# A fourth column group in fp16 pairs, with its high half subtracted by the matrix engine

## The reference

```python
def gnn(x, adj, W, a):                     # called with layernorm(x)
    Wh = x @ W
    e = leaky_relu((Wh @ a[:256])[:, None] + (Wh @ a[256:])[None, :], 0.2)
    e = where((adj > 0) | eye, e, -9e15)
    return softmax(e, axis=1) @ Wh

def ffn(x, Wr, br, ln_g, ln_b, W1, b1, W2, b2):   # called with layernorm(x)
    top_p, top_idx = top_k(softmax(x @ Wr + br), 2)
    weights = top_p / top_p.sum(-1)
    xe = normalised(x) * ln_g[e] + ln_b[e]        # for each expert e
    y = gelu(xe @ W1[e] + b1[e]) @ W2[e] + b2[e]
    return sum of weights * y over the two experts

x = x + gnn(layernorm(x), adj, W, a)
x = x + ffn(layernorm(x), ...)
```

## Time and profile before

| | us |
|---|---|
| median of 3 runs | 986.12 (984.92 to 988.51) |
| the profiled execution's own time | 986.23 |
| its span, first to last instruction | 984.5 |
| PE busy | 950.2 (97%) |
| DVE busy | 780.9 (79%) |
| POOL busy | 687.1 (70%) |
| ACT busy | 615.3 (63%) |

### The profile page before, as it was taken

The page is one execution under the profiler, slowest core; times in us unless marked ns, Lnnn a source line. Parts: engine busy times, 40 slices in busy tenths (PEclk is TensorE's granted clock), DMA queues, the critical chain, the costliest instruction groups (busy, mean ns, idle before and its releaser), DMA issues.

```text
span 984.5 us, 23001 instructions
## 1 busy us (share of the span) xinstructions
PE 950.2 (97%) x7562; PEld 800.1 (81%) x7563; DVE 780.9 (79%) x1199; ACT 615.3 (63%) x905; POOL 687.1 (70%) x726
## 2 busy tenths in 40 slices
PE   6999999999999999999999999999999999999994
PEld 5788999899888998998898977777777777777773
DVE  6789989999999999999999446787666666667653
ACT  4889898897788887977787454333333433343441
POOL 5222261498886987887869558888888888788763
PEclk9999999999999999999999999999999999999998
DMA  9658979688788687886876996442332332233221
GB/s 267 135 158 233 294 229 279 202 270 234 223 254 294 195 287 233 249 263 175 256 273 188 364 356 207 92 114 59 61 56 44 48 59 43 43 48 50 36 43 22
DMA packets 92637, 170.71 MB, mean 173 GB/s; under 512 B 20480, under 2 KB 69888, under 8 KB 84224
## 3 DMA queue, kind: packets, MB, share of 16 engines
q1 hardware_dynamic: 57984, 133.54, 40.6%
q0 software_dynamic: 24048, 26.23, 16.9%
q10 hardware_dynamic: 10512, 9.72, 3.4%
HBM read 136.65 MB, written 41.19 MB: 181 GB/s over the span
## 4 chain that ended last, share of the span: by engine, by line
PE 48%; ACT 1%; issue 1%; DMA 0%; DVE 0%; POOLq 0%; ACTq 0%; DVEq 0%
PE acc L934 12%; PE tp L913 7%; PE tp L915 6%; PE tp L914 6%; PE acc L937 6%; PE acc L807 2%; PE tp L784 2%; PE xt_ps L887 2%; PE acc L804 1%; PE acc L803 1%; PE acc L805 1%; PE rt_ps L827 0%; DMA out<-y_sb,yidx 0%; ACT hf L1177 0%; PE xt_ps L816 0%
## 5 line engine op out<-in xcount | busy, mean ns | idle before, releaser
L566 POOL TENSOR_TENSOR x_late<-x_late,wsp 128x256 f32<-128x256 f32 x128 | 149.6, 1198 | 126.3 <-DMA x_late<-in_L_ffn_W 92.8
L1177 ACT ACTIVATE hf<-tp,b_cols 128x256 f32<-128x256 f32 (+1 forms) x312 | 116.1, 459 | 174.7 <-PE tp L915 172.2
L804 PE MATMUL acc<-wh,pt_hi 128*128 128x256 f16 x768 | 209.3, 273 | 0.0
L803 PE MATMUL acc<-wh,pt_hi 128*128 128x256 f16 x768 | 209.3, 273 | 0.0
L805 PE MATMUL acc<-wh,pt_lo 128*128 128x256 f16 x768 | 209.3, 273 | 0.0
L934 PE MATMUL acc<-w_sb,h_hi 128*128 x568 | 170.9, 379 | 0.7 <-DVE h_lo L1615 0.6
L1311 DVE SCALAR_TENSOR_TENSOR sc<-t_row,s_col 128x2048 f32<-128x2048 f32 x64 | 159.2, 2487 | 10.2 <-PE tp L784 8.3
L913 PE MATMUL tp<-x_hi,w_sb 128*128 128x256 f16 (+1 forms) x624 | 162.4, 264 | 1.9 <-ACT hf L1177 1.8
L673 POOL DMA_INDIRECT out<-y_sb,yidx x71 | 120.7, 1700 | 60.5 <-DVE y_sb L1635 34.4
L915 PE MATMUL tp<-x_down,w_sb 128*128 128x256 f16 (+1 forms) x624 | 162.5, 264 | 0.0
L914 PE MATMUL tp<-x_lo,w_sb 128*128 128x256 f16 (+1 forms) x624 | 161.9, 263 | 0.0
(11 more groups left out here) (238 smaller groups left out, 1785.7 us busy)
## 6 DMA issues: line engine op xcount, KB each, us to landing
adj_sb<-in_adj SPq DMA_DIRECT2D x64, 1024.0 KB, 6.6
x_late<-in_L_ffn_W SPq DMA_DIRECT2D x32, 512.0 KB, 8.2
wsplit_dram<-wsp SPq DMA_DIRECT2D x32, 512.0 KB, 7.0
w_sb<-wsplit_dram SPq DMA_DIRECT2D x32, 512.0 KB, 9.5
xs<-rows_dram ACTq DMA_DIRECT2D x32, 260.0 KB, 3.2
wsp<-in_L_ffn_W POOLq DMA_DIRECT2D x32, 256.0 KB, 5.1
x<-in_x SPq DMA_DIRECT2D x32, 128.0 KB, 8.1
out<-x SPq DMA_DIRECT2D x32, 128.0 KB
```

What stands on the lines that cost most here:

```text
L566: ins = pool.tensor_tensor(wf[q][:, cols], wf[q][:, cols], wsp[q][:, cols], ALU.subtract)
L803: pe.matmul(o, pt_hi[g][:, cols], wh[:, j, 0, :], start=(j == 0), stop=False)
L804: pe.matmul(o, pt_hi[g][:, cols], wh[:, j, 1, :], start=False, stop=False)
```

## The change

The fourth column group is split into fp16 halves like the others, so `Wh` has a low half for all 32 row tiles and `wh32` and `pt32` go. Its low half is not made by DVE. PE subtracts the high half in PSUM: two matmuls of 512 columns with a stationary matrix `minus`, minus the identity divided by 1024, add to the transposed block what `pt_hi[3]` stands for, and ACT copies the remainder (`p_rest`). For this the transposes are written as matmuls with explicit start flags. ACT's and PE's order in a step changes: on PE the products of group 2 of the tile before now stand between the transposes of groups 0 and 1, and the subtraction stands at the end of the step; on ACT `p_rest` comes first, one mask stands between the first two copies, and the weight cast comes after the fourth copy.

The router is spread: two normalisations at q = 1 and two at q = 2, the second half of the logits at q = 3, the position matmuls at the end of the step. They are five, of up to 32 columns, in place of 14 of 8 columns. A one-element gelu on ACT stands ahead of the FFN's first gelu, so that its table is loaded there.

```diff
-        wh32 = sb("wh32", [P, GJ, D], F32, front)
-        pt32 = sb("pt32", [P, GW], F32, front)
+        pt_hi = [sb(f"pt_hi{g}", [P, GW], F16, front) for g in range(G)]
+        pt_lo = [sb(f"pt_lo{g}", [P, GW], F16, front) for g in range(G)]
...
+            pool.tensor_scalar(minus[:, :], ident[:, :], -1.0 / PSCALE, 0.0, ALU.mult, ALU.add).then_inc(s_pc, 1)
...
 project:
-                    pe.wait_ge(s_whl, max(2, 2 * sum(lows[:j - 3])))
+                    pe.wait_ge(s_whl, max(2, 2 * (j - 3)))
 p_transpose:
                 if g == 1 and i > 0:
-                    pe.wait_ge(s_hi, G * i)
+                    pe.wait_ge(s_lq, i)
...
-                    m = pe.transpose(tp[g % 2][...], sc[u][...], ident[:, :])
+                    m = pe.matmul(tp[g % 2][...], sc[u][...], ident[:, :],
+                                  is_transpose=True, start=(g < GS or c % (GJ // 2) == 0), stop=True, skip_group_check=True)
 av:
                 else:
-                    pe.wait_ge(s_hi, G * i + G)
+                    pe.wait_ge(s_lq, i + 1)
...
-                        m = pe.matmul(o, pt32[:, cols], wh32[:, c, :], start=False, stop=(c == GJ - 1))
+                    pe.matmul(o, pt_hi[g][:, cols], wh[:, j, 0, :], start=(j == 0), stop=False)
+                    pe.matmul(o, pt_hi[g][:, cols], wh[:, j, 1, :], start=False, stop=False)
+                    m = pe.matmul(o, pt_lo[g][:, cols], wh[:, j, 0, :], start=False, stop=(j == T - 1))
+            def subtract_high(i):
+                pe.wait_ge(s_hi, G * i + G)
+                for h in range(2):
+                    cols = slice(h * GW // 2, (h + 1) * GW // 2)
+                    m = pe.matmul(tp[1][:, cols], minus[:, :], pt_hi[GS][:, cols], start=False, stop=True, skip_group_check=True)
+                m.then_inc(s_sub, 1)
 router_pos:
+                pe.matmul(rt_ps[:, 64:64 + RB * E], tri[:, :], every_oh, start=True, stop=False, skip_group_check=True)
+                for k in range(1, RB + 1):
+                    m = pe.matmul(rt_ps[:, 64 + k * E:64 + (RB + 1) * E], ones[:, :], every_oh[:, 0:(RB + 1 - k) * E],
+                                  start=False, stop=(k == RB), skip_group_check=True)
 attend on PE:
+                if i > 0:
+                    av(i - 1, 1 - u, 2)
+                if in_batch(b) and q == 3:
+                    router_mm(b, 1)
+                if now:
                     p_transpose(i, u, 1)
                 if i > 0:
-                    av(i - 1, 1 - u, 2)
                     av(i - 1, 1 - u, 3)
...
+                if now:
+                    p_transpose(i, u, 3)
+                    av(i, u, 1)
+                    subtract_high(i)
+                if in_batch(b) and q == 2:
                     router_t(b, 1)
                 if in_batch(b) and q == 3:
                     router_pos(b)
 on ACT:
+            def p_rest(i):
+                act.wait_ge(s_sub, i + 1)
+                if within(i, 1, T):
+                    act.wait_ge(s_av, G * i)
+                act.activation(pt_lo[GS][:, :], tp[1][:, :], ACT.Copy, scale=PSCALE).then_inc(s_lq, 1)
 attend on ACT:
+                if i > 0:
+                    p_rest(i - 1)
+                if in_batch(b) and q == 3:
+                    router(b, 1)
...
                 if ahead:
                     mask(i + 2, u, 0)
+                if now:
+                    p_hi(i, 1)
...
                 if in_batch(b) and q == 2:
                     router(b, 0)
+                if in_batch(b) and (q == 1 or q == 2):
+                    for k in range(2 * (q - 1), 2 * q):
+                        normalise(b, k)
...
                     p_hi(i, 3)
+                    w_scaled(i)
 ahead of the FFN's first gelu, on ACT:
+            act.activation(table_out[:, :], b_cols[0:1, 0, 0:1], ACT.Gelu)
 on DVE, before tile 0:
+            wh_lo(4)
+            wh_lo(5)
             wh_lo(6)
...
-            for j in range(12, NP - 1):
+            for j in range(10, NP - 1):
                 wh_lo(j)
```

More of the change, by code:

```diff
@@ L124, in build @@
         sc = [sb(f"sc{u}", [P, N], F32, front) for u in range(2)]
-        wh = sb("wh", [P, TS, 2, D], F16, front)
-        wh32 = sb("wh32", [P, GJ, D], F32, front)
-        pt_hi = [sb(f"pt_hi{g}", [P, GW], F16, front) for g in range(GS)]
-        pt_lo = [sb(f"pt_lo{g}", [P, GW], F16, front) for g in range(GS)]
-        pt32 = sb("pt32", [P, GW], F32, front)
+        wh = sb("wh", [P, T, 2, D], F16, front)
+        pt_hi = [sb(f"pt_hi{g}", [P, GW], F16, front) for g in range(G)]
+        pt_lo = [sb(f"pt_lo{g}", [P, GW], F16, front) for g in range(G)]
         x_late = sb("x_late", [P, N], F32, front)
@@ L182, in build @@
         xnt_pair += [wsp[1 + p // 2][:, (p % 2) * 4 * D:(p % 2 + 1) * 4 * D].bitcast(F32) for p in range(6)]
-        xnt_pair += [b[:, :].bitcast(F32) for b in pt_hi + pt_lo]
+        xnt_pair += [b[:, :].bitcast(F32) for b in pt_hi[0:GS] + pt_lo[0:GS]]
         late_pairs = [0, 1, 2, 3, 12, 13, 10, 11, 4, 5, 14, 15, 6, 7, 8, 9]
-        lows = [p < 2 * TS // 4 for p in late_pairs]
         side = (xt_ps, rt_ps)
@@ L273, in build @@
         s_lo = sem("p_lo_done")
+        s_sub = sem("p_high_subtracted")
+        s_lq = sem("p_lo_by_act_done")
         s_av = sem("av_done")
@@ L776, in p_transpose @@
                 if g == 1 and i > 0:
-                    pe.wait_ge(s_hi, G * i)
+                    pe.wait_ge(s_lq, i)
                 if g == 1 and i == 0:
-                    pe.wait_ge(s_whl, 2 * sum(lows[:NP - 1]))
+                    pe.wait_ge(s_whl, T - 2)
                     pe.wait_ge(s_whh, T - 2)
@@ L783, in p_transpose @@
                 for c in range(GJ):
-                    m = pe.transpose(tp[g % 2][:, c * P:(c + 1) * P], sc[u][:, (GJ * g + c) * P:(GJ * g + c + 1) * P], ident[:, :])
+                    m = pe.matmul(tp[g % 2][:, c * P:(c + 1) * P], sc[u][:, (GJ * g + c) * P:(GJ * g + c + 1) * P], ident[:, :],
+                                  is_transpose=True, start=(g < GS or c % (GJ // 2) == 0), stop=True, skip_group_check=True)
                 m.then_inc(s_t, 1)
@@ L832, in router_pos @@
                 pe.wait_ge(s_oh, b + 1)
-                for k in range(RB):
-                    o = rt_ps[:, 64 + k * E:64 + (k + 1) * E]
-                    pe.matmul(o, tri[:, :], oh[:, k, :], start=True, stop=(k == 0))
-                    for j in range(k):
-                        pe.matmul(o, ones[:, :], oh[:, j, :], start=False, stop=(j == k - 1))
-                for k in range(RB):
-                    m = pe.matmul(rt_ps[:, 64 + RB * E:64 + RB * E + E], ones[:, :], oh[:, k, :], start=(k == 0), stop=(k == RB - 1))
+                every_oh = oh[:, :, :].rearrange("p k e -> p (k e)")
+                pe.matmul(rt_ps[:, 64:64 + RB * E], tri[:, :], every_oh, start=True, stop=False, skip_group_check=True)
+                for k in range(1, RB + 1):
+                    m = pe.matmul(rt_ps[:, 64 + k * E:64 + (RB + 1) * E], ones[:, :], every_oh[:, 0:(RB + 1 - k) * E],
+                                  start=False, stop=(k == RB), skip_group_check=True)
                 m.then_inc(s_pos, 1)
@@ L863, in attend @@
                     router_pos(b)
-                if now:
-                    p_transpose(i, u, 3)
-                    av(i, u, 1)
-                if in_batch(b) and q == 2:
-                    router_mm(b, 1)
-            pe.wait_ge(s_whl, 2 * sum(lows[:NP - 2]))
+            pe.wait_ge(s_whl, T - 4)
             pe.wait_ge(s_whh, T - 4)
@@ L1042, in p_hi @@
                     act.wait_ge(s_av, G * i + g - 3)
[L1043 to L1044 removed]
+                act.activation(pt_hi[g][:, :], tp[g % 2][:, :], ACT.Copy, scale=PSCALE).then_inc(s_hi, 1)
+            def p_rest(i):
[3 more added lines that the diff above has]
+                act.activation(pt_lo[GS][:, :], tp[1][:, :], ACT.Copy, scale=PSCALE).then_inc(s_lq, 1)
             def normalise(b, k):
@@ L1120, in attend @@
                     exps(i + 1, 1 - u, 1)
-                if in_batch(b) and q == 1:
-                    for k in range(RB):
-                        normalise(b, k)
                 if in_batch(b) and q == 2:
                     router(b, 0)
+                if in_batch(b) and (q == 1 or q == 2):
+                    for k in range(2 * (q - 1), 2 * q):
+                        normalise(b, k)
                 if now:
                     p_hi(i, 2)
-                    w_scaled(i)
                 if ahead:
                     mask(i + 2, u, 1)
-                if in_batch(b) and q == 2:
-                    router(b, 1)
                 if now:
                     p_hi(i, 3)
+                    w_scaled(i)
                 if i == T - 2:
@@ L1153, in _ @@
                 attend(i)
+            p_rest(T - 1)
             def expert_of(t):
```

22 lines of the change are left out of this document (8 added, 14 removed).

## The result

The changed kernel takes 977.32 us (median of four runs, 976.25 to 978.32), the one before 987.32 on the same chip (984.92 to 988.56). The ratio of the two is 0.9902, with a 95% interval of 0.9879 to 0.9924. The forecast was 979, with a range of 970 to 989. The profiled execution took 976.25, with a span of 974.6.

A forecast was written before the change was run, and what follows sets the result against it. PE was taken to set the end, with DVE close behind. From a profiled 986.2 us, attention groups -11.5, start +2.5, end of attention +1.6 and last position matmuls -0.1 gave 978.8, say 979; range 970 to 989.

The forecast's parts named there:

- start, steady part and end: Tile 0 to tile 3, the attention steps after it, attention's last tiles: +2.5, -11.5 and +1.6 us.
- The step laid out: Attention step on PE, ACT and DVE by q, the tile's place in its group of four; 61.8 us per four tiles.
- M: When DVE starts masking, counted from the step's first transpose; forecast -0.5 at q=3, 1.15 at q=0, 1.9 at q=1.
- X: When ACT's exps start in a step: max(5.5, M + 4.5); the fourth high half is ready at X + 7.7.
- rival B: PE alone sets attention's pace: q=1 waits don't appear, PE's idle time goes too, 60.5 per four tiles; 971 us, chance 0.13.
- the two long groups: Four-tile groups of 66.1 and 66.7 us where POOL stretches DVE; forecast 64.2 and 64.4, gains 1.9 and 2.2.
- The threshold: No cover before PE's subtraction when X is over 6.3 (M = 1.8); a plain step has 0.8 us of cover.
- Rival C: ACT behind the subtraction: a late fourth copy stops PE, about 20 steps lose 0.7 us; 993 us, chance 0.16.
- Rival D: Gains are eaten: DVE bound, start and end cost their upper bounds, 7.5 us; 984 us, chance 0.24.
- The end of attention: Tiles 30 and 31: copies stand behind ACT's four tile loads, 2.2 us of idle PE; +1.6 us, bounds 0 and 3.5.
- Position matmuls: Router on PE: 14 take 0.36 us, five wider ones taken as 0.2 (bounds 0.13 and 0.36), moved after the subtraction.
- Early table: FFN start: PE's 1.83 us wait is for the second tile's split x, not the table load; worth 0, at most -1.3.

The follow-up runs named there:

- e7: The changed kernel with POOL's four weight-split subtractions per tile cut to one of eight columns: 966.71 us, ratio 0.9794 to the kernel before.
- e3: The changed kernel with ACT's weight cast put back before the fourth copy: 987.53 us, ratio 1.0007 to the kernel before.
- e2: The kernel before with only the router part (split normalisations, moved logits half, five position matmuls at step end): 977.02 us, ratio 0.9901.
- e1: The changed kernel with its router put back as before, so fourth group and new step order alone: 985.7 us, ratio 0.9993 to the kernel before.
- e12: The kernel before with only the five position matmuls, at the end of the step: 986.96 us, ratio 1.0008.
- e9: e2 with POOL's weight-split subtractions cut to one of eight columns: 972.44 us, ratio 0.9854 to the kernel before.
- e4: The changed kernel without the one-element gelu that loads the table early: 976.8 us, ratio 0.9898 to the kernel before.

## Why the prediction was right, and where it was not

**The time** was right, 979 against 977.3, and so was the division into start, steady part and end: +2.5, -11.5, +1.6 forecast, +2.0, -12.1, +0.5 measured (and -0.3 in the FFN). Each came out a little under its forecast, so that the span fell by 9.9 us for 7.4.

**The step laid out** was right in most of its kinds, and at q = 1 by luck. Plain step 14.43 forecast, 14.41 measured; q = 2 16.2 and 16.12; q = 3 15.45 and 15.38; q = 1 15.7 and 14.7 to 16.3. A q = 0 step was to have no wait, 14.43, and took 14.4 to 15.9.

The sums of the prediction do not give its 15.7. It lets DVE start masking 1.15 us into a q = 0 step; its own numbers, -0.5 + 13.7 + 2.7 - 15.45, give 0.45. With that, q = 1 has M = 1.2 and X = 5.7, the low half is in time, and the subtraction waits about 0.4: 14.8. This is what e7 shows with POOL quiet, 14.75 at q = 1, 14.44 at q = 0 and 60.7 for each group of four, close to the 60.5 of rival B. In the kernel after, DVE starts masking 1.2 to 2.7 us into the q = 0 steps from tile 8 on, and two of the three groups forecast at 61.8 measured 61.7 and 61.8, because POOL's meetings with DVE are in them too. The prediction added these to the two long groups only, and the value of 1.15 took their place in the others.

The threshold was right as well: e3 crosses it with 0.9 us and loses 10.2. The q = 1 wait of the subtraction (0.34 us, forecast 0.5) looks like this, on ACT and then on PE, tile 13:

```profile
268.17 1.08 ACT L1067 ACTIVATE rows<-x,nb,rs 128x256 f32<-128x256 f32 x2
...
271.95 1.00 ACT L1053 ACTIVATE pt_hi<-tp 128x1024 f16<-128x1024 f32 x1
```

```profile
273.01 0.61 PE L815 MATMUL tp<-pt_hi,minus 128*128 128x512 f16 x2 [0.34 <-ACT pt_hi L1053]
```

**What the change gains it by** was wrong, and this is the step that failed. The largest gain that the prediction prices is the fourth group's, 0.41 us per tile and 13.1 over 32. Of the router part it calls "the place" of the position matmuls important, and it names the four normalisations only as a part of the idle time of the two long groups. The runs show otherwise. The router part alone makes the whole 10 us (e2), the group alone nothing (e1), the positions alone nothing (e12). I laid out the step of after with care, and never laid out the step of before with one edit in it; the split normalisations stood in my ACT queue as an entry of 1.0 us, without the question of what the other 1.0 had cost. The trace had it: the step of tile 14 was 18.9 us long behind the earlier trace rows. The total came out right because it was the difference between two whole schedules, and for that no attribution is needed.

**Rival B** (971, the group's saving in full and the idle time gone too) did not happen while POOL works. PE's idle time of tiles 3 to 30 went from 9.1 us in the kernel before to 2.4 in e2, and with the group back to 9.9. **Rival C** did not happen in the change as made, but it is what e1 and e3 show: their 9.5 and 15.2 us of waits for the fourth high half. **Rival D** had the right mechanism for the group: its saving was eaten by a DVE that is stretched while POOL works. e7 and e9 show it (8.0 us of worth with POOL quiet, 1.5 with POOL). D's number was wrong in its other half: it puts the start and the end at their upper bounds, 7.5 us, and they cost 2.5.

**The rule weighed.** The rule of the Trainium skill (SBUF — State Buffer, "Who interferes with whom"), that these two engines exclude each other when both read SBUF in this way, taken strictly, would have put the sum 4 us higher, as collisions keep their price in a shorter step. I kept 1.9 and 2.2 us of gain for the two long groups, and measured they gained 3.4 and 3.2, so the sum by that reading was further off. The collisions did not keep their price because the two worst did not occur again: the longest score of the kernel after is 2.81 us, and DVE's busy time over tiles 4 to 30 is 399.9 us for 405.5. For the group alone the reasoning was right: e9 and e7 show 3.5 us of POOL's price reaching PE at 14.8 us per step and 10.1 at 14.4.

**Terms that were mis-sized.** The end of attention: +0.5 for +1.6. ACT and PE near tile 31:

```profile
544.40 1.02 ACT L1059 ACTIVATE pt_lo<-tp 128x1024 f16<-128x1024 f32 x1 [4.30 <-issue]
```

```profile
545.97 1.06 PE L835 MATMUL rt_ps<-w_r_sb,xnt_b 128*128 128x8 f32 x8 [0.89 <-ACT xnt_b L1086]
```

The wait that I put at 2.2 us is 0.89. ACT fell idle for the loads at 540.10 (544.40 less 4.30), 14.8 us into tile 30's step; before it was 549.26 (553.92 less 4.66), 16.4 into the step. There the exps of the step started 7.8 us into it, for 5.7 after, and the second router copy stood ahead of the loads too. I had taken the loads at their old place. The groups of tiles 12 to 15 and 24 to 27 came 1.5 and 0.9 us shorter than forecast, those of 16 to 19 and the last three tiles 0.9 and 1.3 longer: POOL meets DVE in other steps than before, and I had added the meetings of before at their old places. The start was +2.0 for +2.5.

**Position matmuls**, five wider ones taken as 0.2 us (the row between the two, with the other four, is left out):

```profile
557.83 0.18 PE L842 MATMUL rt_ps<-oh,tri 128*128 128x32 bf16 x1
...
557.95 0.63 PE L897 MATMUL xt_ps<-ident,xs 128*128 128x128 f32 x4
```

They take 0.12 (557.83 to 557.95), just under my lower bound of 0.13.

**Early table** was worth 0, as said: e4. The load stands in a gap of ACT in the trace of after, and the PE wait at the FFN's start (1.83 in the earlier trace rows) is still there at 571.33, now 1.82:

```profile
563.05 1.28 ACT L1202 ACT_TABLE_LOAD   x1
```

```profile
571.33 0.28 PE L923 MATMUL tp<-x_hi,w_sb 128*128 128x256 f16 x1 [1.82 <-issue]
```

## What to carry to other kernels

When a change has several parts, lay out the old step with each part alone, not only the new step with all: a right total says nothing about which part earned it. Here the part that was largest on paper earned nothing by itself, and moving small router work on ACT and PE came with the whole gain. A saving on the busiest engine is worth only the room of the next one, and that room has to be read with the other engines' interference in it: 15.0 us of stretching on DVE cost 3.5 us at 14.8 us per step, and 16.0 cost 10.1 at 14.4. And where two engines disturb each other, an edit elsewhere can make the worst meetings come or go, so look for them in both traces before the gain is put down to the edit. A wait that is taken away alone may only have been hiding the next one behind it (e12).

## What the runs showed of the hardware

**Either engine can pay for a meeting.** In the earlier trace rows POOL's four pieces began at 251.98, the score at 252.06, and the score took 4.63 us for 2.34. In the kernel after, tile 12 again, DVE and then POOL:

```profile
241.13 2.56 DVE L1331 SCALAR_TENSOR_TENSOR sc<-t_row,s_col 128x2048 f32<-128x2048 f32 x1
...
251.16 2.34 DVE L1331 SCALAR_TENSOR_TENSOR sc<-t_row,s_col 128x2048 f32<-128x2048 f32 x1
```

```profile
239.62 4.61 POOL L568 TENSOR_TENSOR x_late<-x_late,wsp 128x256 f32<-128x256 f32 x4 [0.87 <-DMA wsp<-in_L_ffn_W]
...
252.12 3.81 POOL L568 TENSOR_TENSOR x_late<-x_late,wsp 128x256 f32<-128x256 f32 x4 [1.08 <-DMA wsp<-in_L_ffn_W]
```

Here the score of 251.16 began first and takes its bare 2.34 us, and the four pieces from 252.12 take 3.81 for 2.56. The score of 241.13 began while the third of four pieces ran. It lost 0.2 us, and it was the fourth piece, begun 0.38 us after the score, that grew to 2.71 us:

```profile
241.51 2.71 POOL L568 TENSOR_TENSOR x_late<-x_late,wsp 128x256 f32<-128x256 f32 x1
```

So DVE came in between two pieces here, while in the earlier trace rows it lost 2.3 us, nearly the whole run of four. What decides this the traces do not show. Over the whole span POOL's sum rose from 149.6 to 161.0 us and the mean score fell from 2487 to 2378 ns. That the instruction that starts first is the one that keeps its time is read from these rows alone and was not tested by itself.

**Smaller pieces take POOL longer.** 256 pieces of 128 columns took 233.1 us in sum and 128 of 256 columns 161.7; a piece of half the width costs 943 ns against 1293 in the mean. The medians are 423 and 672 ns, so two small ones take 0.17 us more than one large one even there. The rest of both sums is in pieces that took longer than that.
